# Second feed-forward layer of the short path: products of halves in place of full-precision products

## The reference, cut to what matters

```
h  = modulate(layernorm(attention(x) @ proj_w + proj_b), shift_msa, scale_msa)
x  = x + gate_msa * h
g  = gelu(x @ fc1_w + fc1_b)                 # 512 x 1024, exact gelu
y  = g @ fc2_w + fc2_b                       # 512 x 256
x  = x + gate_mlp * modulate(layernorm(y), shift_mlp, scale_mlp)
```

## Time and profile before

| | us |
|---|---|
| median of 3 runs (lowest, highest) | 1373.91 (1371.72, 1375.23) |
| the profiled execution, its own time | 1371.17 |
| its span | 1369.4 |
| TensorE busy | 1287.7 (94%) |
| VectorE, ScalarE, GpSimd busy | 786.8, 744.8, 754.1 |

### The profile page before, as it was taken

How to read it: one execution, slowest core, us unless ns; L and a number is a source line. 1 busy time by engine, 2 the same in 40 slices (tenths; PEclk the granted TensorE clock), 3 DMA queues, 4 the chain that set the end, 5 groups by cost and what they waited for, 6 DMA issues and landing times. The chain is left out here.

```text
span 1369.4 us, 24388 instructions
## 1 busy us (share of the span) xinstructions
PE 1287.7 (94%) x8725; PEld 993.0 (73%) x8725; DVE 786.8 (57%) x2223; ACT 744.8 (54%) x1246; POOL 754.1 (55%) x939
## 2 busy tenths in 40 slices
PE   4899999999999999999999999799999999999888
PEld 3567778778778778778778777667777677776656
DVE  3766845845845845845844744546655566564552
ACT  3466674674674674674674774354445444444431
POOL 3688876876876866866866865101224042240423
PEclk9999999999999999999999999999999999999998
DMA  8532231231331341340340330727243452434100
GB/s 263 146 101 81 63 116 45 74 116 38 81 116 34 80 121 29 78 127 18 79 136 15 104 128 18 234 70 218 68 163 118 126 170 70 160 105 124 48 2 31
DMA packets 98259, 133.98 MB, mean 98 GB/s; under 512 B 16802, under 2 KB 51498, under 8 KB 98130
## 3 DMA queue, kind: packets, MB, share of 16 engines
q1 hardware_dynamic: 96850, 131.80, 32.6%
q10 hardware_dynamic: 1280, 0.53, 0.2%
HBM read 72.64 MB, written 58.75 MB: 96 GB/s over the span
## 5 line engine op out<-in xcount | busy, mean ns | idle before, releaser
L1418 DVE CUSTOM_DVE_ANT_0 shifted<-score,bias 128x512 f32<-128x512 f32 x512 | 332.1, 686 | 279.5 <-PE score L880 200.6
L635 POOL TENSOR_SCALAR shifted<-shifted,row_max 128x512 f32<-128x512 f32 x512 | 363.8, 724 | 169.1 <-DVE row_max L1418 166.2
L1126 ACT ACTIVATE probs<-turned 128x512 f32<-128x512 f32 x512 | 277.7, 595 | 218.9 <-PE turned L892 218.8
L892 PE MATMUL turned<-ident,shifted 128*128 128x128 f32 x2048 | 269.6, 274 | 4.7 <-ACT probs L1126 4.6
L892 PEld LDWEIGHTS turned<-ident,shifted 128*128 128x128 f32 x2048 | 232.7, 141 | 56.5 <-issue 33.0
L804 PE MATMUL dense<-w_down,hidden 128*128 128x256 f32 x1024 | 261.8, 382 | 2.4 <-ACT hidden L1107 2.4
L628 POOL TENSOR_SCALAR bias<-dist,scale 128x1024 f32<-128x1024 f32 x192 | 215.5, 1123 | 13.4 <-DMA down_bias<-in_L_cond_b 13.4
L880 PE MATMUL score<-k_rows,q_rows 97*128 97x512 f32 x512 | 202.0, 456 | 12.6 <-DMA k_rows<-mask_neg 3.7
L804 PEld LDWEIGHTS dense<-w_down,hidden 128*128 128x128 f32 x1024 | 178.1, 190 | 37.1 <-issue 9.6
L784 PE MATMUL dense<-feat_m,w_up 128*128 128x512 f32 x768 | 192.2, 402 | 9.7 <-DVE feat_m L1375 9.6
L784 PEld LDWEIGHTS dense<-feat_m,w_up 128*128 128x128 f32 x768 | 143.9, 192 | 42.5 <-issue 11.8
(11 more groups left out here) (140 smaller groups left out, 1461.2 us busy)
## 6 DMA issues: line engine op xcount, KB each, us to landing
qk_rows<-qk_high SPq DMA_DIRECT2D x128, 256.0 KB
q_rows<-qk_rows SPq DMA_DIRECT2D x64, 384.0 KB
qk_rows<-qk_low SPq DMA_DIRECT2D x64, 256.0 KB
k_rows<-qk_rows SPq DMA_DIRECT2D x68, 192.0 KB
x_in_t<-in_x SPq DMA_DIRECT2D x8, 512.0 KB, 4.6
x_res<-in_x SPq DMA_DIRECT2D x8, 512.0 KB, 5.6
x_mid<-x_norm SPq DMA_DIRECT2D x8, 512.0 KB, 3.2
x_in_t<-x_mid SPq DMA_DIRECT2D x8, 512.0 KB, 4.0
```

What stands on the lines that cost most here:

```text
L635: ins = pool.tensor_scalar(shifted[:, u % 3, i, :], shifted[:, u % 3, i, :], -1.0, row_max[:, t % 6:t % 6 + 1], ALU.mult, ALU.add)
L892: mm = pe.transpose(turned_bank[z % 2][:, HALF * kk + P * i:HALF * kk + P * i + P], shifted[:, u % 3, i, P * kt:P * kt + P], ident[:, :])
L1126: act.activation(probs[:, u % RING, 2 * pair:2 * pair + 2, :], turned_bank[z % 2][:, :].rearrange("p (a c) -> p a c", a=2), ACT.Exp)\
L1418: dve.tensor_tensor_reduce(shifted[:, u % 3, i, :], score_bank[t % 2], bias[:, u % 2, i, :], 1.0, 3.0e38, ALU.add, ALU.min, row_max[:, t % ...
```

## The change

In the short path each chunk of `down` becomes three products of halves. For this

- ScalarE copies each gelu piece to `hidden_high` right after it has written it, waiting for its own gelu, and VectorE writes `hidden - hidden_high` to `hidden_low(c)` at the steps of HEADS_LOW: piece 0 at step 10, ahead of `take_peaks`; 1 and 2 at step 11; 3 to 6 at step 13, ahead of `take_peaks`; 7 at step 17.
- `hidden_low(c)` has no tile of its own: it is row c % 4 of `qk_high` (c below 4) or `qk_low`. Before it writes there, VectorE waits until the stores of that row for pass n + 1 have landed (`halves_stored`), except in the last turn and the epilogue, where no such stores are.
- the weights are split once, in turn 9: `take_down_high` on ScalarE after step 8, `take_down_low` on VectorE at step 11.
- `probs` becomes two tiles, and `down_high`, `hidden_high` and `down_low` are laid over `bias`, the second `probs`, `w_out` and `w_down`, which the first block alone uses in full.
- TensorE's `down_chunks` waits for `low_ready` chunk by chunk in place of the last gelus.

```diff
+    HEADS_LOW = {10: (0,), 11: (1, 2), 13: (3, 4, 5, 6), 17: (7,)}
...
-        w_out = sb("w_out", [P, 2, DC, D], F32R)
-        w_down = sb("w_down", [P, FCH, D])
-        bias = sb("bias", [P, 2, 2, L])
-        probs = sb("probs", [P, RING, TT, HALF])
+        probs = [sb("probs0", [P, RING, 2, HALF])]
+        with ExitStack() as first:
...
+            bias = first_sb("bias", [P, 2, 2, L])
+            probs.append(first_sb("probs1", [P, RING, 2, HALF]))
+            w_out = first_sb("w_out", [P, 2, DC, D], F32R)
+            w_down = first_sb("w_down", [P, FCH, D])
+        down_high = sb("down_high", [P, FCH, D], F32R)
+        hidden_high = sb("hidden_high", [P, FCH, L], F32R)
+        down_low = sb("down_low", [P, FCH, D], F32R)
+        def hidden_low(c):
+            return (qk_high, qk_low)[c // 4][:, c % 4, :]
...
 TensorE, down_chunks
+                    if short(m):
+                        if i == 0 and c == 0:
+                            pe.wait_ge(s["down_split"], 1)
+                        if i == 0:
+                            pe.wait_ge(s["low_ready"], FCH * (m - B) + c + 1)
...
+                    if short(m):
+                        left = (hidden_high[:, c, :], hidden_low(c))
+                        right = (down_high[:, c, :], down_low[:, c, :])
+                        for x, y in TERMS:
+                            mm = pe.matmul(bank_of(piece, m)[:, 0:D], left[x][:, P * i:P * i + P], right[y],
+                                           start=(c == 0 and (x, y) == TERMS[0]),
+                                           stop=(c == FCH - 1 and (x, y) == TERMS[-1]))
...
 ScalarE, dense, after the gelu
+                    if short(m):
+                        piece_read(act, piece, m)
+                        act.activation(hidden_high[:, i, :], hidden[:, i, :], ACT.Copy).then_inc(s["high_ready"], 1)
...
 VectorE
+            def take_hidden_low(m, c):
+                if m + 2 < N:
+                    dve.wait_ge(s[f"halves_stored{c % 4 // 2}"], STORED * (m + 3))
+                dve.wait_ge(s["high_ready"], FCH * (m - B) + c + 1)
+                dve.tensor_tensor(hidden_low(c), hidden[:, c, :], hidden_high[:, c, :].bitcast(F32),
+                                  ALU.subtract).then_inc(s["low_ready"], 1)
...
                         for piece, m in pieces(HEADS, 3 * p + 1, n):
                             dense(piece, m)
+                        if n > B:
+                            for c in HEADS_LOW.get(3 * p + 1, ()):
+                                take_hidden_low(n - 1, c)
                         if 2 <= p < 2 + H // 2:
                             take_peaks(n, p - 2)
                         for piece, m in pieces(HEADS, 3 * p + 2, n):
                             dense(piece, m)
+                        if n == B + 1 and p == 3:
+                            take_down_low()
+                        if n > B:
+                            for c in HEADS_LOW.get(3 * p + 2, ()):
+                                take_hidden_low(n - 1, c)
```

More of the change, by code:

```diff
@@ L198, in build @@
         out_whole = v_ext[:, 0, :, :].rearrange("p h e -> p (h e)").rearrange("p (c n) -> p c n", c=DC)
-        bias = sb("bias", [P, 2, 2, L])
         no_bias = sb("no_bias", [P, L])
-        probs = sb("probs", [P, RING, TT, HALF])
-        head_probs = probs[:, :, 0:2, :].rearrange("p r a b -> p r (a b)")
+        probs = [sb("probs0", [P, RING, 2, HALF])]
+        head_probs = probs[0][:, :, :, :].rearrange("p r a b -> p r (a b)")
         head_out = sb("head_out", [P, 2, HALF])
@@ L222, in build, with first_sb @@
         mask_colf = sb("mask_colf", [P, TT])
-        staged = probs[:, :, :, :].rearrange("p a b c -> p (a b c)")
+        with ExitStack() as first:
+            def first_sb(name, shape, dt=F32):
+                return first.enter_context(nc.sbuf_tensor(name, shape, dt))
+            bias = first_sb("bias", [P, 2, 2, L])
[7 more added lines that the diff above has]
+            return (qk_high, qk_low)[c // 4][:, c % 4, :]
+        staged, staged_too = (x[:, :, :, :].rearrange("p a b c -> p (a b c)") for x in probs)
         raw_qkv = staged[:, 0:6 * D].rearrange("p (c n) -> p c n", c=DC)
@@ L229, in build @@
                    dist[:, 0, :].rearrange("p (c n) -> p c n", c=DC)]
-        raw_up = [staged[:, 8 * D:16 * D].rearrange("p (c n) -> p c n", c=DC),
+        raw_up = [staged_too[:, 0:8 * D].rearrange("p (c n) -> p c n", c=DC),
                   bias[:, :, :, :].rearrange("p c a b -> p c (a b)")]
@@ L265, in build @@
                  "y_scaled", "y_done", "last_ready", "tile_stats0", "tile_stats1", "tile_mean0", "tile_mean1", "tile_var0",
-                 "tile_var1", "tile_rstd0", "tile_rstd1")
+                 "tile_var1", "tile_rstd0", "tile_rstd1", "down_taken", "down_split", "high_ready", "low_ready")
         s = {name: sem(name) for name in names}
@@ L797, in down_chunks @@
                     piece = ("down", i)
-                    if i == 0 and c == 0:
+                    if short(m):
[3 more added lines that the diff above has]
+                            pe.wait_ge(s["low_ready"], FCH * (m - B) + c + 1)
+                    elif i == 0 and c == 0:
                         for last_up in range(DENSE):
@@ L803, in down_chunks @@
                         bank_free(pe, piece, m)
-                    mm = pe.matmul(bank_of(piece, m)[:, 0:D], hidden[:, c, P * i:P * i + P],
-                                   w_down[:, c, :], start=(c == 0), stop=(c == FCH - 1))
+                    if short(m):
[5 more added lines that the diff above has]
+                                           stop=(c == FCH - 1 and (x, y) == TERMS[-1]))
+                    else:
+                        mm = pe.matmul(bank_of(piece, m)[:, 0:D], hidden[:, c, P * i:P * i + P],
+                                       w_down[:, c, :], start=(c == 0), stop=(c == FCH - 1))
                     if c == FCH - 1:
@@ L908, in attend @@
                                        v_ext[:, kt, HG * (gq // 2) + j, :],
-                                       probs[:, (4 * gq + j) % RING, kt, :], start=(kt == 0), stop=(kt == TT - 1),
+                                       probs[kt // 2][:, (4 * gq + j) % RING, kt % 2, :], start=(kt == 0), stop=(kt == TT - 1),
                                        skip_group_check=True)
@@ L1108, in dense, with take_down_high @@
                                    bias=up_bias[:, i:i + 1]).then_inc(used(piece, m), 1)
+                    if short(m):
+                        piece_read(act, piece, m)
+                        act.activation(hidden_high[:, i, :], hidden[:, i, :], ACT.Copy).then_inc(s["high_ready"], 1)
+            def take_down_high():
+                act.wait_ge(s["down_loaded"], 96)
+                act.wait_ge(s["up_split"], 2)
+                act.activation(down_high[:, :, :], w_down[:, :, :], ACT.Copy).then_inc(s["down_taken"], 1)
             def make_bias(n, u):
@@ L1125, in exps @@
                     act.wait_ge(s["turned_ready"], TILES * n + z + 1)
-                    act.activation(probs[:, u % RING, 2 * pair:2 * pair + 2, :],
+                    act.activation(probs[pair][:, u % RING, :, :],
                                    turned_bank[z % 2][:, :].rearrange("p (a c) -> p a c", a=2), ACT.Exp)\
@@ L1197, in turn @@
                             dense(piece, m)
+                        if n == B + 1 and p == 2:
+                            take_down_high()
                         if n == B and p == 6:
@@ L1242, in take_qkv_low, with take_down_low @@
                     .then_inc(s["qkv_split"], 1)
+            def take_down_low():
+                dve.wait_ge(s["down_taken"], 1)
+                dve.tensor_tensor(down_low[:, :, :], w_down[:, :, :], down_high[:, :, :].bitcast(F32), ALU.subtract)\
+                    .then_inc(s["down_split"], 1)
+            def take_hidden_low(m, c):
[4 more added lines that the diff above has]
+                                  ALU.subtract).then_inc(s["low_ready"], 1)
             def norm_stats(m, i, src):
@@ L1596, in epilogue @@
                         dense(piece, m)
+                        if piece[0] == "up":
+                            take_hidden_low(m, piece[1])
                         if piece == ("wout", TT - 1):
```

## The result

The kernel after takes 1402.74 us (median of four runs, 1401.46 to 1403.23), the kernel before in the same comparison 1372.82 (1371.65 to 1375.23). The ratio is 1.0217, with a 95% interval of 1.0205 to 1.0229: slower by 30 us. The forecast was 1406, range 1388 to 1422. The profiled execution took 1402.86 with a span of 1401.0, 31.6 more than the span before.

The account below looks back on a forecast made before the run. TensorE's program order, nearly back to back, threaded by a per-head-pair chain, was taken as the bound. +32.8 (wait) - 6 x 1.4 (products) - 1.3 (turn 15) - 3.2 (tail) + 12 (clock) = +32: forecast 1406, range 1388 to 1422.

Parts of the forecast that it names:

- The wait: VectorE before half 2, turns 9 to 14: waiting for stores delays pair 3's scores 5.2 us a turn, 32.8 in all.
- The estimate of 2.6 us: Last store's landing after its issue, from fixed 2.0 us plus bytes over 436 GB/s; delay some 2.8 us a turn.
- the prologue's row: SP waited 5.0 us for six like stores in the prologue; basis for landing 5.04 us after issue ends.
- The clock: TensorE's 5.5 us stand in turns 9 to 14 drops the clock to 1.2 GHz: 2 us a turn, 12 in all.
- Rival A: The wait costs as forecast, but the clock stays up because the stand is split in two: +20, 1394; chance 15%.
- The products: Second layer on TensorE: three products of halves save 0.078 us a step; 1.4 us a turn in turns 9 to 14.
- turn 15: The turn without the wait, as no next-but-one sequence follows: -1.3 us.
- the tail: Last sequence's second layer: 2.5 us saved by products, start 0.7 earlier, -3.2 us in all.
- The added work: ScalarE's copies (0.63 us each), VectorE's subtractions (0.67 each) and the weight split fit beside TensorE: 0 us.
- rival D: VectorE is not held at half 2, as the stores land before its reduction for pair 2: -11.5, 1362; chance 6%.
- D's other condition: The same faster outcome, 1362, would come if VectorE could go past the waiting instruction.
- Sum: All terms against the profiled execution: +32 us, giving 1403 for that execution and 1406 as forecast.

Follow-up runs that it names:

- e3: Kernel before plus only VectorE's wait for halves_stored1 ahead of the reduction for pair 2, full-precision products, no halves: 1393.56 us, ratio 1.0147.
- e8: The change with its rows and wait, only halves 3 to 6 moved behind the peaks of pair 2 (step 14): 1388.84 us, ratio 1.0111.
- e2: The change with its rows and wait, but halves 2 to 5 made at step 14 and half 6 at step 16: 1369.82 us, ratio 0.9977.
- e4: The change with unread products keeping TensorE busy in its two stands, ten before pair 2's transpose, seven before pair 3's scores: 1390.39 us, ratio 1.012.
- e5: The change's products and weight split without the hidden layer's copies, subtractions and store waits; second layer's values not computed: 1361.44 us, ratio 0.9912.
- e1: The change with low halves written into the hidden layer's own rows, so no wait for stores: 1373.68 us, ratio 1.0001.
- e6: e1 with subtractions moved to steps where GpSimd is idle (0 to 4 at step 13, 5 at 14, 6 at 16): 1362.31 us, ratio 0.9916.
- e7: e1 with GpSimd's four 128x1024 operations released by the last piece of the first layer instead of the first: 1401.26 us, ratio 1.0208.
- e9: e6 with unread products keeping TensorE busy in existing stands in turns 8 and 15 and the epilogue: 1357.11 us, ratio 0.9881.

## Why the prediction was right

**The wait (+32.8 in the sum).** The step is right in mechanism and nearly in size: the scores of pair 3 were 5.2, 6.3, 4.9, 4.6, 6.3 and 5.3 us late in turns 9 to 14, 32.7 in all. Half 2 started 26.3 us into turn 12, and I had put it at 26.3 (1122.2 less 1095.9). The scores of pair 3 were 4.6 us late there against 5.2, since the halves follow each other every 0.6 us and not 0.67. (The store landed 4.7 us after its issue and not 5.04, but its issue ended 0.3 us later in the turn.) e3 shows the 2.2 us of the wait by itself, e8 that halves 3 to 6 ahead of the peaks carry most of the rest, e2 that the waiting instruction costs little where VectorE comes to it after the landing and with nothing urgent behind it. The landing is not one number: in the six turns, from the end of the last issue to the start of half 2, it was 5.9, 6.6, 5.2, 4.7, 6.6 and 5.8 us. The estimate of 2.6 us that I had worked out from the Trainium skill (DMA: Bandwidth & Descriptors, Anatomy of one DMA) for a transfer by itself is too small in all six, as the prologue's row had said. That section gives its figures for transfers that GpSimd issues, which the prediction did not say; these are issued by SyncE, with others still in the queue.

**What the step left out.** Half 0 waits as well, for the stores of the first two pieces: 2.97 us in turn 13, 1.16 in turn 12. In turns 10 and 13 this delays pair 2 by 2.4 us and pair 3 to 32.7. On the other side turn 9 was not later than the others (5.2 us where 6.8 was said), because its last store was issued 19.7 us into the turn (947.58 less 927.9) and not 21.2, as before. The two misses nearly cancel, and that is luck.

**The clock (+12).** Right in mechanism, and in size within 2 us: 12.3 between the medians of the change and e4, some 10.5 by the turns. The fall came in every turn, for 6.8 us in five and 3.4 in one (turn 13, where it lay ahead of the scores of pair 3 and cost nothing behind them). In turn 12 it begins 0.6 us before the end of the first stand, and a good part of it lies in the second stand, which is why the stretch costs 1.6 us in that turn (pair 3 to pair 4, against e4) and not 3.4. Rival A (1394, clock stays) is what e4 measured at 1390.4, and needs dummy products to be true. The rule by which I called the fall certain (the Trainium skill, TensorE: Matmul & The Clock Gate, What's actually happening) is borne out for these stands; of e3's shorter ones two in six passed without a fall, so it is not certain for every stand.

**The products (-12.9 with turn 15 and the tail).** e5 measures -11.7 for all of them. 1.4 us a turn was said and 1.4 found; in the change turn 15 gave 1.0 against 1.3. In the change itself the part of turn 12 behind the scores of pair 3 takes 30.5 us as before (1148.96 to 1179.5, against 1122.45 to 1153.0), with 3.5 us of it at half clock, which cost 1.75: so the products gave about 1.7 there. The tail is 4.7 us shorter, of which 1.7 are a stretch of 6.8 us at half clock in place of 10.2; 3.0 remain against 3.2: 2.6 by the products, and some 0.3 by the earlier start, where 2.5 and 0.7 were said.

**The added work (0).** Right in the change, for a reason that I did not give. A half cost 0.67 to 0.81 us by the earlier trace rows; on `qk_high` rows it cost 1.38, since GpSimd's three operations of 128x1024 run at that time. In the change this is mostly inside the time that VectorE then waits for the stores anyway. Take the wait away (e1), and the same halves hold the chain, for 11.4 us more than in e6. Out of GpSimd's way, all the copies and subtractions cost 0.9 us (e6 against e5). So rival D, the change without any wait, at 1362, is wrong for the place where the halves stand (1373.7) and right for another place (1362.3). VectorE not going past a waiting instruction, on which D's other condition hung, agrees with e3, where the reduction behind the wait starts at 26.3 us or later in every turn: the Trainium skill's strict order (TensorE: Matmul & The Clock Gate, Architectural detail: the array is 16× 32×32) is what it shows.

**Sum.** In the profiled execution: +34.6 in turns 9 to 14, where -8.4 + 32.8 + 12 = 36.4 was said, -1.0 (-1.3), -4.7 (-3.2), and +2.7 ahead of turn 9, which the prediction does not have. That last goes with more time at half clock than in the execution before: twice 6.8 us around turn 8 against twice 3.4, and 6.8 against 3.4 at 43 us. It is not the change's: e3 is the kernel before up to turn 9, and its profiled execution has the same stretches at half clock and starts turn 9 at 927.7. Seven of the nine other kernels had 10.2 to 13.7 us of it around turn 8, and two 6.8, as before. The 1406 was 3 us above the median: 2 from the sum (32 against 30 by medians), 1 because the median that I started from was 1 us higher than that of this comparison.

**Open.** Why stands of 2.2 to 2.3 us made the clock fall in two turns of e3 and not in two others. Why the stores land 4.7 us after their issue in one turn and 6.6 in the next; GpSimd's work and the loads beside them were not varied. The order of the 32 chunks was left as it is, and a new one was not tried.

## What to carry to other kernels

A wait costs what stands behind it on its engine: when a buffer is reused, list the instructions that follow the wait in program order and who waits for them, and move what is urgent ahead of it; here an edit of one table was worth 33 us (e2). VectorE and GpSimd can hold each other without a wait in the profile, so when an operation goes to a new place, compare its duration there with its duration elsewhere, and look at what GpSimd runs beside it. Where TensorE has a stand that can't be removed, products that nobody reads can keep its clock up, and cost nothing while they lie inside the stand.

## What the runs showed of the hardware

- A VectorE subtraction of 128x512, 0.69 us alone, takes up to 2.9 us beside GpSimd operations of 128x1024 (2.4 us each; e1), and one of 128x8 takes 2.22 instead of 0.17 (e7). It ends 0.55 us after GpSimd's operation (0.02 for the small one). Reductions and scalings that read PSUM were not affected.
- The granted clock fell to 0.50 for 3.4 us behind one stand of 2.21, 2.23, 2.61 or 3.76 us, and did not behind 2.19 and 2.28 (e3). With two stands of 4.3 us together it fell for 6.8 us (the change, turn 12).
- Filling the stands with products took 12.3 us off one kernel (the change to e4; some 10.5 of it the clock) and 5.2 off another (e6 to e9).
- The last of twelve stores of 256 KB, issued at intervals of 0.6 to 1.7 us, landed 4.7 to 6.6 us after the end of its issue (the change, six turns).
- A product of halves of 128x256 with a new weight block takes 0.118 us where nothing else is in the way, 0.213 at half clock, against 0.432 for the two records of a full-precision one.
